# Neighbour counts: VectorE adds the first eight edge tiles of a half to the last eight, TensorE counts over the eight sums

## The reference, cut to what matters

```python
h = x @ Wt.T + bt                                    # 4096 x 64
s = leaky_relu(h @ Wa.T + ba, negative_slope=0.2)    # one number per node (row)
scores = where(adj > 0, s, NEG)                      # s of the row itself, or NEG
w = softmax(scores, axis=1)
y = x + (w @ h) @ Wp.T + bp                          # then a layer norm with gamma, beta
```

## Time and profile before

| | |
|---|---|
| median of 3 runs | 1323.04 us (1322.70 to 1323.28) |
| the profiled execution | 1323.13 us |
| its span, first to last instruction | 1321.3 us |
| TensorE busy | 1206.2 us (91%) |
| VectorE busy | 1114.5 us (84%) |
| last stage (from 1183 us), the counts alone (L722) | 256 matmuls |

### The profile page before, as it was taken

How to read it: one execution, slowest core, us unless ns; L and a number is a source line. 1 busy time by engine, 2 the same in 40 slices (tenths; PEclk the granted TensorE clock), 3 DMA queues, 4 the chain that set the end, 5 groups by cost and what they waited for, 6 DMA issues and landing times.

```text
span 1321.3 us, 32008 instructions
## 1 busy us (share of the span) xinstructions
PE 1206.2 (91%) x12034; PEld 352.4 (27%) x12050; DVE 1114.5 (84%) x1583; ACT 1056.9 (80%) x1200; POOL 883.8 (67%) x924
## 2 busy tenths in 40 slices
PE   5655999999999999999999999999999969998995
PEld 3331111111111111111111111111111126874542
DVE  6765999999999999999999999999999964642344
ACT  4544999999999999999999999999999944431000
POOL 5674777777777777777777777777777743531223
PEclk9776999999999999999999999999999978999998
DMA  5002222432233232333223322333232246306850
GB/s 171 1 0 96 99 97 97 135 123 97 97 114 131 110 113 97 111 130 113 97 97 120 138 97 97 113 127 115 97 113 107 94 156 228 120 1 232 308 201 25
DMA packets 41020, 152.47 MB, mean 115 GB/s; under 512 B 5088, under 2 KB 19232, under 8 KB 30624
## 3 DMA queue, kind: packets, MB, share of 16 engines
q1 hardware_dynamic: 36640, 148.26, 31.6%
q10 hardware_dynamic: 4224, 2.10, 0.5%
HBM read 110.50 MB, written 39.85 MB: 114 GB/s over the span
## 4 chain that ended last, share of the span: by engine, by line
ACT 63%; PE 19%; issue 7%; DVE 5%; POOL 3%; POOLq 1%; DMA 0%; DVEq 0%; ACTq 0%; SPq 0%
ACT probs L1072 36%; ACT probs L1066 27%; PE ps L711 4%; PE ps L661 2%; PE ps L718 2%; PE ps L670 2%; POOL probs L972 2%; PE ps L1275 2%; DVE probs L1175 2%; PE ps L722 1%; PE ps L1215 1%; DVE probs L1113 1%; DVE acc_sb L1183 1%; PE ps L635 1%; PE ps L749 1%
## 5 line engine op out<-in xcount | busy, mean ns | idle before, releaser
L1175 DVE SCALAR_TENSOR_TENSOR probs<-m,ps 128x512 f32<-128x512 bf16 (+1 forms) x1024 | 928.5, 950 | 34.0 <-PE ps L1275 15.4
L1072 ACT ACTIVATE probs<-probs 128x1536 f32<-128x1536 f32 x512 | 868.2, 1697 | 0.9
L1008 POOL TENSOR_TENSOR probs<-probs,m 128x512 f32<-128x512 f32 x512 | 596.0, 1164 | 226.8 <-ACT probs L1066 197.7
L1288 PE MATMUL ps<-probs,v_sb 128*17 128x512 f32 x4096 | 539.2, 599 | 0.2 <-ACT probs L1072 0.2
L1275 PE MATMUL ps<-kq 32*128 32x512 bf16 x6144 | 426.9, 380 | 37.1 <-DVE probs L1175 9.7
L1066 ACT ACTIVATE probs<-ps 128x512 f32<-128x512 f32 x512 | 411.8, 804 | 23.8 <-PE ps L1275 23.1
L1275 PEld LDWEIGHTS ps<-kq 32*128 32x128 bf16 x6144 | 114.7, 93 | 564.4 <-ACT probs L1066 499.1
L987 POOL TENSOR_SCALAR m<-adj_in 128x512 bf16<-128x512 int32 x256 | 157.4, 615 | 4.0 <-issue 4.0
L1288 PEld LDWEIGHTS ps<-probs,v_sb 128*17 128x17 f32 x4096 | 68.2, 95 | 219.1 <-issue 210.6
L422 ACT ACTIVATE adj_in<-ps 128x512 f32<-128x512 f32 x8 | 4.8, 598 | 94.8 <-PE ps L722 94.8
L711 PE MATMUL ps<-kq,probs 128*128 128x512 bf16 x240 | 56.8, 386 | 3.8 <-DVE probs L514 2.9
(11 more groups left out here) (134 smaller groups left out, 642.8 us busy)
## 6 DMA issues: line engine op xcount, KB each, us to landing
adj_in<-in_adj_t SPq DMA_DIRECT2D x64, 1024.0 KB, 5.6
mask_t<-m SPq DMA_DIRECT2D x64, 512.0 KB, 2.9
kq<-mask_t SPq DMA_DIRECT2D x16, 2048.0 KB, 7.9
attn_t<-acc_sb SPq DMA_DIRECT2D x16, 256.0 KB, 6.5
probs<-in_x SPq DMA_DIRECT2D x12, 256.0 KB, 4.0
tail_words<-attn_t SPq DMA_DIRECT2D x4, 512.0 KB, 4.1
probs<-attn_t SPq DMA_DIRECT2D x4, 512.0 KB, 3.6
out<-m ACTq DMA_DIRECT2D x8, 256.0 KB, 3.5
```

Of the source, the lines that this page charges most:

```text
L1008: nc.gpsimd.tensor_tensor(pr, pr, m01[:, (k // 2) % MRING, :], ALU.mult).then_inc(postmasked, 1)
L1072: nc.scalar.activation(pr, pr, ACT.Exp, scale=UNIT).then_inc(exped, 1)
L1175: nc.vector.scalar_tensor_tensor(out=pr, in0=m.to_broadcast([P, n, CH]), scalar=1.0, in1=ps[:, b:b + n, :], op0=ALU.subtract, op1=ALU.add)\
L1288: last = nc.tensor.matmul(ps[RT * hh:RT * hh + VW, 6 + g, :], v_sb[:, t, h * VW:(h + 1) * VW], probs[:, k % SLOTS, hh // 2, (hh % 2) * CH: ...
```

## The change

VectorE adds the first eight tiles of each half to its last eight, in bf16 (`pair_sums`, one instruction for a half, 128 x 4096 elements; the sums are 0, 1 or 2). TensorE multiplies the column of ones with the eight sum tiles in place of the sixteen edge tiles (`degrees`). The sums have two buffers, on a part of `q_shift`, which nothing else uses there. The counts leave `sums_low`; `degrees` of a half now stands behind `sums_high` of the next one. A half is free for the next load when `sums_low` and `pair_sums` are both through. ScalarE's copy of the counts gets a semaphore of its own.

```diff
@@ load_edges
             sp.wait_ge(edges_used, n - ERING + 1)
+            sp.wait_ge(pairs_made, n - ERING + 1)
@@ tail_scalar, for each block j
                 if j > 0:
                     act.wait_ge(y_done, j)
+                act.wait_ge(pairs_used, 2 * j + 2)
                 nc.scalar.activation(deg_sb, ps[:, BANK_D[j % 2], :], ACT.Copy).then_inc(deg_copied, 1)
@@ tail_vector
+            def pair_sums(n):
+                dve.wait_ge(edges_in[n % ERING], 16 * (n // ERING + 1))
+                if n >= 2:
+                    dve.wait_ge(pairs_used, n - 1)
+                nc.vector.tensor_tensor(pairs[n % 2], edges[:, n % ERING, 0:HALF // 2, :],
+                                        edges[:, n % ERING, HALF // 2:HALF, :], ALU.add).then_inc(pairs_made, 1)
...
             dve.wait_ge(row_step, 3)
+            pair_sums(0)
+            pair_sums(1)
             dve.wait_ge(csw_made, 1)
...
             for j in range(NC):
                 add_parts(j)
+                if j + 1 < NC:
+                    pair_sums(2 * j + 2)
                 weights(j)
                 residual(j)
+                if j + 1 < NC:
+                    pair_sums(2 * j + 3)
                 finish(j)
@@ tail_tensor, sums_high
                 if half == 0 and j >= 2:
                     pe.wait_ge(s_made, j - 1)
-                    pe.wait_ge(deg_copied, j - 1)
@@ sums_low
-                    nc.tensor.matmul(ps[r:r + HID, BANK_B[j % 2], :], h3[:, t, 2 * HID:3 * HID],
-                                     edges[:, n % ERING, t % HALF, :], start=t < 2, stop=t >= NT - 2)
-                for t in range(half * HALF, (half + 1) * HALF):
+                    last = nc.tensor.matmul(ps[r:r + HID, BANK_B[j % 2], :], h3[:, t, 2 * HID:3 * HID],
+                                            edges[:, n % ERING, t % HALF, :], start=t < 2, stop=t >= NT - 2)
+                last.then_inc(edges_used, 1)
+
+            def degrees(n):
+                j, half = n // 2, n % 2
+                pe.wait_ge(pairs_made, n + 1)
+                if half == 0 and j >= 2:
+                    pe.wait_ge(deg_copied, j - 1)
+                for t in range(HALF // 2):
                     r = (t % 4) * RT
-                    last = nc.tensor.matmul(ps[r:r + RT, BANK_D[j % 2], :], one_col[:, :],
-                                            edges[:, n % ERING, t % HALF, :], start=t < 4, stop=t >= NT - 4)
-                last.then_inc(edges_used, 1)
+                    last = nc.tensor.matmul(ps[r:r + RT, BANK_D[j % 2], :], one_col[:, :], pairs[n % 2][:, t, :],
+                                            start=half == 0 and t < 4, stop=half == 1 and t >= HALF // 2 - 4)
+                last.then_inc(pairs_used, 1)
@@ the order
             sums_high(1)
             sums_low(1)
+            degrees(0)
             column_sums()
             for j in range(1, NC):
                 sums_high(2 * j)
+                degrees(2 * j - 1)
                 sums_low(2 * j)
                 project_sums(j - 1)
                 sums_high(2 * j + 1)
+                degrees(2 * j)
                 sums_low(2 * j + 1)
+            degrees(2 * NC - 1)
             project_sums(NC - 1)
```

More of the change, by code:

```diff
@@ L142, in gnn_kernel @@
         acc_stored = sem("acc_stored")
+        HALF = NT // 2
         def taker(*areas):
@@ L162, in gnn_kernel @@
         m_words = m01[:, :, :].rearrange("p s q -> p (s q)").bitcast(F32)
-        wb = taker(pool_words, v_words, adj_words, m_words)
+        q_words = q_shift[:, :, :].rearrange("p g n -> p (g n)").bitcast(F32)
+        wb = taker(pool_words, v_words, adj_words, m_words, q_words)
         lb = taker(tail_words)
@@ L186, in gnn_kernel @@
         den, aw, ew = wb(SUB), wb(SUB), wb(SUB)
+        pairs = [wb(HALF * CH // 4).bitcast(BF16).rearrange("p (t q) -> p t q", q=CH) for _ in range(2)]
         BANK_A, BANK_B, BANK_D = (0, 3), (1, 4), (5, 7)
         NM = FF // P
-        HALF = NT // 2
         ERING = 5
@@ L211, in gnn_kernel @@
         edges_in = [sem(f"edges_in{u}") for u in range(ERING)]
-        edges_used = sem("edges_used")
+        edges_used, pairs_made, pairs_used = sem("edges_used"), sem("pairs_made"), sem("pairs_used")
         row_step, e_made = sem("row_step"), sem("e_made")
```

## The result

| | us |
|---|---|
| before, 8 runs beside it | 1323.30 (1322.49 to 1323.51) |
| changed, 8 runs | 1319.57 (1318.34 to 1320.32) |
| ratio | 0.9972, 95% interval 0.9961 to 0.9983 |
| forecast | 1318.2, range 1315.8 to 1321.8, faster 80% |

The change makes the kernel 3.7 us faster, 0.3% of its time. Of these 4.2 about 1.0 arose ahead of the change: the last piece of h starts at 1187.40 here and at 1189.39 before, 1.99 earlier, of which the counts of half 0 explain 0.98.

The account below looks back on a forecast made before the run. The prediction took TensorE to bound the last stage's blocks. From 1323.13 us it took 7.84 for counts, added 2.24 for the last pair sum and 0.7 for the clock: 1318.2 us, range 1315.8 to 1321.8.

Parts of the forecast that it names:

- The bound: Last stage: TensorE's time is the block's time, 14.64 us before and 13.66 after, with no wait inside a block.
- What TensorE saves: Counts before the next-to-last projection: 15 x 0.98 becomes 14 x 0.49, saving 7.84 us (6.86 with 0.56 a group).
- The pair sum: VectorE's bf16 sum of 4096 elements a partition takes 2.2 us, with 4.4 as upper end.
- The root is held: GpSimd's root does not run under VectorE's pair sum; its 1.41 us stand behind it, end chain +2.24 us.
- VectorE keeps up: VectorE's work between two projections takes 12.8 us, under TensorE's 13.66, with 0.9 to spare.
- The new waits: Semaphore waits for pair sums and counts' copy are hidden in the blocks; TensorE waits about 2.7 us at the end.
- The clock at the end: Last projection may run at granted clock 0.50 after TensorE's wait: 0.7 us taken, about a one-in-two chance of 1.4.
- 1: GpSimd's root runs under the pair sum, so the end chain grows by only 0.83 us: 1316.5 us; 15%.
- 2: VectorE becomes the bound between projections, pair sum 4.4 us: 1341 us, or 1327 with the root under it; 10%.
- 3: GpSimd's gamma and beta steps both precede the second pair sum, block 14.1 us: 1320.9 us; 5%.
- 4: On TensorE, eight counts cost nearly what sixteen do, 0.70 us a group, saving 4.9: 1321.2 us; 8%.
- The sum: Whole kernel: 1323.13 - 7.84 + 2.24 + 0.7 = 1318.2 us; this forecast had 62%.

Follow-up runs that it names:

- e4: Changed kernel without pair sums: sixteen count matmuls a half over the edge tiles, at their new place; 1322.01 us, ratio to before 0.9996.
- e7: Changed kernel plus one VectorE sum of half as many bf16 elements with an f32 result; executed once, that sum at 1.1 ns an element.
- e5: Changed kernel with each pair sum computed twice, one after the other; 1344.42 us, ratio to before 1.0169.
- e3: Changed kernel with 14 idle matmuls in TensorE's two waits before the last projection; 1316.80 us, ratio to before 0.9964.
- e2: Changed kernel with only half 15 undone: sixteen count matmuls over edge tiles, no pair sum; 1315.70 us (ratio 0.9954), beside e8 1315.48 (0.9939).
- e8: e2 plus 10 idle matmuls in TensorE's wait before half 1 at the stage's start; 1314.04 us, ratio to before 0.9930.

## Why the prediction was right, point by point

- **The bound.** Right: TensorE alone sets the block before and after, and it waits for nothing inside one.
- **What TensorE saves.** Right in kind, mis-sized in its term for the counts: 15 x 0.98 - 14 x 0.55 = 7.0 us instead of 7.84. The 0.56 kept for the range was the value: two rounds at the pace of the high sums (0.43) and an entry of 0.13 give it. Of the 7.0, 6.0 (14 x 0.43) are the halved matmuls and 0.98 the order (e4). The trace shows 6.9 saved up to the end of the next-to-last projection.
- **The pair sum.** 2.26 us against 2.2, which hung on a single one-input f32 row; e7's trace shows that it takes bf16 on both sides, inputs and result. The estimate of 2.3 from the Trainium skill ("VectorE: DVE Perf Modes", The perf-mode tier table) was a little nearer.
- **The root is held.** Right (2.16 in place of 0.20), with one detail missed: it ends with the pair sum instead of starting behind it, so that 1.20 of the 1.41 us stand behind, and the end grew by 1.97 instead of 2.24.
- **VectorE keeps up.** Forecast 0.9 us to spare, measured 1.29. e5 shows what a block costs when VectorE does not keep up.
- **The new waits.** Right: TensorE waits for a pair sum only once, 0.92 us for that of half 15, outside the blocks. The wait behind the last counts is 2.29 us; forecast about 2.7.
- **The clock at the end.** Right in kind, mis-sized: 0.7 was a half chance, the fall came in both traces of the changed kernel, at 1.74. e3 shows the mechanism. The wait of 2.87 us that the prediction argues from the earlier trace rows probably holds a matmul whose record is missing (x15 there): at the same place every other trace without a filling has 2.47 or 2.48.
- **The rivals.** 1 is out: the root's first step lasts as long as the pair sum. 2 is out: 2.26 us, not 4.4. 3 is out: the beta step (L344) is held beside the second pair sum, 3.20 us, and does not go ahead of it. 4 is out: a group costs 0.55, not 0.70.
- **The sum.** -4.9 forecast; +0.84 for the counts, +1.04 for the clock and -0.27 for the end make -3.3. The last stage of the traces shows 3.2, the medians 3.7 and, the second time, 3.3. That the first traced execution lies only 0.7 above the forecast is in part luck: 1.0 us of its gain arose ahead of the change.

## What to carry to other kernels

Here work moved from the busy engine to one that waited was free in the steady blocks and paid for at the last one, where the chain runs over that engine: there leave it undone (e2). When a wait of TensorE grows at such a place, ask also what its clock does to the short work behind it; idle matmuls in the wait bought back 1.7 us in the traces, at each of two places (e3, e8). And the time that an engine has to spare is used up by more than the new operations' own length: of 7.0 us a block 1.29 are left after two sums of 2.26, since the block became shorter and GpSimd's reads hold the second sum up. When the medians of two versions differ by 2 or 3 us, lay their traces side by side from the last place that both have in common: that parts what the edit did from what wandered ahead of it.

## What was not expected of the hardware

- At granted clock 0.50 the last projection, eight f32 matmuls of one column and eight of 128, took 1.86 + 1.93 us against 1.05 + 1.01: it nearly doubles, and their weight loads with it (PEld busy 3.49 us against 1.85 in e3).
- A held GpSimd operation shows as busy (2.16 and 3.20 us), not as waiting; only its duration beside the same operation's elsewhere tells.
- The changed kernel's executions spread over 2.0 and 2.7 us, those of before over 1.0 in the first comparison, and 4.2, 1.6 and 1.2 beside the experiments. Filling the waits did not narrow them (e3: 2.2). In the traced executions the place that wandered lies ahead of the last stage (1.6 us in the table above, against 0.1 behind it); what wanders there stays open.
